# A fused two-layer image network on one core: the last phase's norm terms made in four rounds a unit

## The chip, the cores and the metric

The kernel runs on one core of a Trainium2 chip. The metric is the device time of one execution in microseconds (us), lower is better. TensorE (PE) does matrix products and transposes, VectorE (DVE) and ScalarE (ACT) work on tiles of 128 partitions, GpSimd (POOL) does small work beside them, and SyncE (SP) issues the DMAs. Each engine runs its own instructions in order; engines wait for each other by semaphores.

## The reference, cut to what matters

The input is an image batch of 8 x 96 channels x 128 x 128. The function has two layers, each of them a mixing part and a token-wise feed-forward part:

```
# layer 0
x = x + cluster_mixing(ln_c(x))                      # pooled centres, similarities
t = tokens(x);  t = t + ffn0(ln_t(t));  x = image(t)
# layer 1
n = ln_c(x) * gamma + beta                           # norm over the 96 channels
y = conv1x1(conv5x1(conv1x5(conv3x3(n))))            # depthwise, then 96x96
x = x + y * n
t = tokens(x)                                        # 131072 tokens of 96 channels
t = t + ffn1(ln_t(t))                                # output
# ln_t(v) = (v - mean) / sqrt(var + 1e-5), over the 96 channels of a token
# ffn(v): fp8 (5,2) rounded input and weights, 96 -> 384, + b1, relu,
#         rounded to fp8, 384 -> 96, + b2
```

The change touches only the norm `ln_t` ahead of the last feed-forward. For each token it needs a factor `rstd = (var + eps) ** -0.5` and an offset `shift = -mean * rstd`; the normalised token is `x * rstd + shift`.

## The kernel before, in words

The program has three phases, one after the other. Phase A does layer 0 and the norm of layer 1, phase B the depthwise convolutions, and phase C (function `phase_c`, names beginning `C_` in the profile) the rest: the 1x1 convolution, the product, the residual, and the second feed-forward. Only phase C is changed.

Phase C cuts the work into 32 units (`NQ`), each a quarter of one image, 4096 tokens. A unit is 32 tiles of 128 tokens (`NT`), in 8 groups k = 0 to 7 (`NK`) of 4 tiles each (`TPC`). The code of every engine walks over steps. In a step, unit i goes through the feed-forward, and unit q = i + 1 goes through the front part: convolution (`mix`, PE), product (`gate`, DVE), transpose to tokens (`turn`, PE), residual (`x4`, DVE, tile `C_xT`), statistics (`stats`, DVE, the BATCH_NORM_STATS2 of L178, tile `C_st`). A step has nine slots s = 0 to 8. The order on each engine is written out by hand in its `body`. With its names in the profile, what one slot s holds is:

- PE: `pe_q8(s+1)` (transpose of the normalised tokens, L1519), two thirds of `pe_hidden(s)` (L357), `mix(s)` (L1738), the last third of `pe_hidden(s)`, `pe_y(s-1)` (L1533), `turn(s-1)` (L1747), `c_turn(s-1)` (L1757).
- ACT: `act_q8(s+1)` (C_q8c, L305), three `act_hidden(s)` (C_h, L370), one group of the norm `act_norm` (C_q, L1504, four instructions, one for each tile), `act_y(s-1)` (C_y, L1546).
- DVE: `dve_hidden(s)` (C_hq, three of L378 and one of L382), `gate(s)` (L1822), `x4(s-1)` (L1832), `dve_y(s-1)` (C_y16b, L1552), `stats(s-1)` (L178, two), `out(s-1)` (C_outq, L1851).

Which group ACT normalises in which slot stands in a table. Groups 0, 1 and 2 of the next unit are normalised in slots 6, 7 and 8 of a step, groups 3 to 7 in slots 0 to 4 of the following one, and slot 5 has none:

```
LN_AT = {6: (1, 0), 7: (1, 1), 8: (1, 2), 0: (0, 3), 1: (0, 4), 2: (0, 5), 3: (0, 6), 4: (0, 7)}
```

POOL has one task in phase C, `norm_terms(q, half)`: from the statistics of half a unit (16 tiles, groups 0 to 3 or 4 to 7) it makes `rstd` and `shift`. It waits until DVE has finished the statistics of the half's last group (semaphore `bn2`), until ACT has used up the half's terms of the unit before (`norm2`), and for its own round before (`ln2`). Then it issues four instructions that depend on each other: var (L1891), less (L1892), pow (L1895, tile `C_rstd`), and shift (L1898). The last raises `ln2`. ACT waits for `ln2` ahead of groups 0 and 4, and DVE ahead of the statistics of groups 0 and 4 (they overwrite what the round of the unit before has read). The statistics of group 3 come in slot 4 of a step, those of group 7 in slot 8, the last one. So the terms of the second half can be started only as the step ends, and ACT reads them in slot 1 of the next step.

A counter `passed` is raised by POOL and ACT behind each such wait; nobody waits for it. SP loads the image rows (`C_x3q`, `C_y3q`) three steps ahead and the tokens (`C_xT`) two steps ahead.

Of the kernel before, what the change touches and what calls it, by code (L numbers as in the profile page):

```python
# [11 lines left out]
ALU = mybir.AluOpType  # L12
# [4 lines left out]
B, C, H, W = 8, 96, 128, 128  # L17
# [5 lines left out]
NT = TOK // P  # L23
NK = 8
TPC = NT // NK
# [7 lines left out]
EPS_T = 1e-5  # L33
# [71 lines left out]
def begun(unit):  # L105

    return unit.real
# [68 lines left out]
def pair_stats(dve, st, x, n):  # L176

    return dve.bn_stats(st[:, n:n + 2, :].rearrange("p t s -> p (t s)"),  # L178
                        x[:, n * C:(n + 2) * C].rearrange("p (t c) -> p c t", t=2))
# [1299 lines left out]
class RowFeedForward(SplitFeedForward):  # L1479
# [15 lines left out]

    def act_norm(self, act, i, k):
        ev = self.ev
        if k % 4 == 0:

            act.wait_ge(ev["ln2"], ev.at("ln2", i, k // 4))  # L1500
            act.sem_inc(ev.passed, 1)
        x = self.x_of(i)
        for t in range(k * TPC, (k + 1) * TPC):
            m = act.activation(self.q8[:, t, :], x[:, t * C:(t + 1) * C], ACT.Identity,  # L1504
                               scale=self.rstd[:, t:t + 1], bias=self.shift[:, t:t + 1], saturate=False)
        m.then_inc(ev["norm2"], 1)
# [108 lines left out]
def phase_c(nc, bufs, y3_dram, out_dram):  # L1615
# [3 lines left out]
    with ExitStack() as ctx:  # L1619
# [3 lines left out]
        for s in range(FFN_SLOTS):  # L1623
# [6 lines left out]
            if s >= 1:  # L1630
                front_uses.append(("turn", s - 1, 1, "x1", s - 1))
                back_uses += [("y", s - 1, 0, "y16", s - 1), ("c", s - 1, 0, "out", s - 1)]
        ev = Events(nc, ctx, "C_", dict(x1=NK, bn2=NK, ln2=2, ln2_s=6, norm2=NK, q8_full=NK, y_full=NK, c_full=NK, q8c=NK,
                                        hidden=NJ * NK, h16=NJ * NK, relu=NK, hq=NK, y16=NK, yb=NK, out=NK, pw_full=NK,
                                        turn_full=NK, gate=NK, out_st0=1, out_st1=1))
        NB, HR = LastBuffers.NB, RB // 2
# [3 lines left out]
        cst, idb, pw, expo, var, less = bufs.cst, bufs.idb, bufs.pw, bufs.expo, bufs.var, bufs.less  # L1640
# [4 lines left out]
        ff = RowFeedForward(nc, ctx, "C_", ev, back, xT_flat, wts, idb)  # L1645

        def group(plane, k):

            return plane[0:C, (k // 2) * 8:(k // 2) * 8 + 8, (k % 2) * QS:(k % 2) * QS + QS]
# [7 lines left out]
        def rows(flat):  # L1657

            return flat.rearrange("c (r w) -> c r w", w=QS)

        def steps(eng, body):
            for n in range(-1, NQ):
                body(Unit(0, n, 4, NQ - 1))
# [140 lines left out]
        @block.vector  # L1804
        def _(dve):
            dve.wait_ge(setup, 32)
            dve.tensor_copy(idb[:], cst[:]).then_inc(setup_dve, 1)
            dve.memset(expo[:], -0.5).then_inc(setup_dve, 1)
            ffn_dve(dve)

            def gate(q, k):

                dve.wait_ge(ev["pw_full"], ev.at("pw_full", q, k))
                if k == 0:

                    dve.wait_ge(ld_x[q.buf(2)], (q.round(2) + 1) * 16)

                if k >= 2:
                    dve.wait_ge(ev["turn_full"], ev.at("turn_full", q, k - 2))
                elif begun(q - 1):  # L1820
                    dve.wait_ge(ev["turn_full"], ev.at("turn_full", q - 1, NK - 2 + k))
                dve.tensor_tensor(rows(gated[:, k % 2, :]), rows(front.bank("pw", k)[0:C, 0:CH])[:, ::-1, :],  # L1822
                                  group(x3q[q.buf(2)], k), ALU.mult).then_inc(ev["gate"], 1)

            def x4(q, k):
                if k == 0:

                    dve.wait_ge(ld_t[q.buf(NB)], (q.round(NB) + 1) * 32)

                dve.wait_ge(ev["turn_full"], ev.at("turn_full", q, k))  # L1830
                v = xT[q.buf(NB)][:, k, :]
                dve.tensor_tensor(v, front.bank("turn", k)[:, 0:CW], v, ALU.add).then_inc(ev["x1"], 1)  # L1832

            def stats(q, k):
                if k % 4 == 0 and begun(q - 1):

                    dve.wait_ge(ev["ln2"], ev.at("ln2", q - 1, k // 4))
                dve.wait_ge(ev["x1"], ev.at("x1", q, k))
                for t in range(0, TPC, 2):
                    m = pair_stats(dve, ff.st, ff.x_of(q), k * TPC + t)  # L1840
                m.then_inc(ev["bn2"], 1)

            def out(i, k):
                if k % 4 == 0 and begun(i - 1):

                    n = f"out_st{k // 4}"
                    dve.wait_ge(ev[n], ev.at(n, i - 1, 0) * 16)

                dve.wait_ge(ev["c_full"], ev.at("c_full", i, k))
                dve.wait_ge(ev["yb"], ev.at("yb", i, k))  # L1850
                dve.tensor_tensor(group(outq, k), rows(back.bank("c", k)[0:C, 0:CH]), rows(ff.y16b[:, k % 2, :]),  # L1851
                                  ALU.add).then_inc(ev["out"], 1)

            def body(i):
                q = i + 1
                for s in range(FFN_SLOTS):
                    if i.real and s < NK:
                        ff.dve_hidden(dve, i, s)
                    if q.real and s < NK:
                        gate(q, s)  # L1860
                    if q.real and s >= 1:
                        x4(q, s - 1)
                    if i.real and s >= 1:
                        ff.dve_y(dve, i, s - 1)
                    if q.real and s >= 1:
                        stats(q, s - 1)
                    if i.real and s >= 1:
                        out(i, s - 1)

            steps(dve, body)  # L1870

        @block.gpsimd
        def _(pool):
            pool.wait_ge(setup_dve, 2)

            def norm_terms(q, half):

                n = NT // 2
                o = half * n
                pool.wait_ge(ev["bn2"], ev.at("bn2", q, 4 * half + 3))  # L1880
                pool.sem_inc(ev.passed, 1)
                if begun(q - 1):

                    pool.wait_ge(ev["norm2"], ev.at("norm2", q - 1, 4 * half + 3))
                    pool.sem_inc(ev.passed, 1)

                earlier = q if half else q - 1
                if begun(earlier):
                    pool.wait_ge(ev["ln2"], ev.at("ln2", earlier, 1 - half))
                    pool.sem_inc(ev.passed, 1)  # L1890
                pool.tensor_scalar(var[:], ff.st[:, o:o + n, 2], 1.0 / C, EPS_T, ALU.mult, ALU.add).then_inc(ev["ln2_s"], 1)  # L1891
                pool.tensor_scalar(less[:], ff.st[:, o:o + n, 1], -1.0, 0.0, ALU.mult, ALU.add).then_inc(ev["ln2_s"], 1)  # L1892
                pool.wait_ge(ev["ln2_s"], ev.at("ln2_s", q, 3 * half + 1))
                pool.sem_inc(ev.passed, 1)
                pool.tensor_tensor(ff.rstd[:, o:o + n], var[:], expo[:, 0:n], ALU.pow).then_inc(ev["ln2_s"], 1)  # L1895
                pool.wait_ge(ev["ln2_s"], ev.at("ln2_s", q, 3 * half + 2))
                pool.sem_inc(ev.passed, 1)
                pool.tensor_tensor(ff.shift[:, o:o + n], less[:], ff.rstd[:, o:o + n], ALU.mult).then_inc(ev["ln2"], 1)  # L1898

            def body(i):  # L1900
                q = i + 1
                for half in range(2):
                    if q.real:
                        norm_terms(q, half)

            steps(pool, body)


def metaformer_kernel(nc, x, consts, wf_t, wf, bf, wv_t, bv, wp_t, bp, alpha, beta, w1_0, b1_0, w2_0, b2_0,
                      gamma, beta_ln, dw13, valid, dwb, pw_t, w1_1, b1_1, w2_1, b2_1, out):  # L1910
    x2_dram = nc.dram_tensor("x2_scratch", [NQ, P, NK * CW], F32, kind="Internal").ap()
    x3_dram = nc.dram_tensor("x3_scratch", [C, B, H, W], F32, kind="Internal").ap()
    y3_dram = nc.dram_tensor("y3_scratch", [C, B, H, W], F32, kind="Internal").ap()
    strip_dram = nc.dram_tensor("strip_scratch", [C, 3, TAPW], F32, kind="Internal").ap()
    edge_dram = nc.dram_tensor("edge_scratch", [C, 2, 3, P], F32, kind="Internal").ap()
    phase_a(nc, consts, x, wf_t, wf, bf, wv_t, bv, wp_t, bp, alpha, beta, w1_0, b1_0, w2_0, b2_0,
            gamma, beta_ln, dw13, strip_dram, edge_dram, x2_dram, x3_dram)
    with ExitStack() as ctx:
        bufs = LastBuffers(nc, ctx, consts, pw_t, w1_1, b1_1, w2_1, b2_1, x2_dram, x3_dram)
        phase_b(nc, valid, dwb, strip_dram, edge_dram, x3_dram, y3_dram, bufs)  # L1920
        phase_c(nc, bufs, y3_dram, out)
# [54 lines left out]
```

## Time and profile before

| | us |
|---|---|
| median of 3 runs | 3664.3 (3664.11 to 3664.59) |
| the profiled execution, its own time | 3659.49 |
| its span in the trace | 3657.6 |
| busy: DVE, PE, ACT, POOL | 3218.4, 3017.4, 2781.3, 1728.9 |

The page also has the whole span in 40 slices. Phase C fills the last 12 of them: DVE and ACT are busy 90% or more in nearly all of those, PE 80%, POOL 20%. The chain that ended last, over the whole span, passes through ACT for 16%, through DVE for 4% and through POOL for 4%; the POOL part is the pow (C_rstd, L1895, 3%) with what stands around it. A busy share says how full an engine is on average; which wait ends last in a place has to be read from the timeline and the chain there.

### The profile page before, as it was taken

What the parts mean: (1) busy time and instruction counts of PE and PEld (TensorE: products, weight loads), DVE (VectorE), ACT (ScalarE), POOL (GpSimd) and SP (SyncE); (2) the same over time, 40 slices, a digit from 0 to 9 for tenths busy, and PEclk for the clock granted to TensorE, in tenths of its full rate; (3) what the DMA queues carried; (4) which work ended last, traced back from release to release, by engine and by line L of the source; (5) the groups of instructions that cost most, each with busy time, mean ns of one, the idle gap of its engine ahead of it and who ended that gap; (6) DMA issues with size and microseconds to landing.
All of it is one profiled execution on the core that took longest, in us unless ns stands there. A gap on an engine that the chain in (4) does not pass through costs nothing. (4 is left out here: it accounts for less than half of the span.)

```text
span 3657.6 us, 68122 instructions
## 1 busy us (share of the span) xinstructions
PE 3017.4 (82%) x21990; PEld 1910.0 (52%) x21990; DVE 3218.4 (88%) x8131; ACT 2781.3 (76%) x6274; POOL 1728.9 (47%) x2404
## 2 busy tenths in 40 slices
PE   6787888878787878887876799997888888888887
PEld 5565665656565656565654344443444444444444
DVE  4888889898989898989886699999899999999998
ACT  2577777777777877777778455554799999999998
POOL 3777777777787877787864000000222222222221
PEclk9999999899999999999987899999999999999999
DMA  3233323232323232323212888897676667666762
GB/s 68 53 89 74 91 71 88 71 88 70 88 71 88 71 88 71 88 71 88 71 56 69 212 238 234 236 280 212 172 199 188 181 185 200 184 184 193 199 177 83
DMA packets 696178, 478.92 MB, mean 131 GB/s; under 512 B 407217, under 2 KB 674422, under 8 KB 683830
## 3 DMA queue, kind: packets, MB, share of 16 engines
q1 hardware_dynamic: 695830, 474.58, 49.2%
q8 instruction: 182, 2.98, 0.3%
q14 instruction: 166, 1.36, 0.1%
HBM read 272.09 MB, written 201.92 MB: 130 GB/s over the span
## 5 line engine op out<-in xcount | busy, mean ns | idle before, releaser
L1891 POOL TENSOR_SCALAR C_var<-C_st 128x16 f32<-128x16 f32 x64 | 13.5, 211 | 1338.6 <-DVE C_st L178 1338.6
L1464 DVE SCALAR_TENSOR_TENSOR B_y<-B_mid,B_coefs,B_y 128x512 f32<-128x512 f32 x768 | 509.0, 750 | 3.2 <-ACT B_y L1429 3.2
L1395 PE MATMUL B_ps_row<-B_z,B_band 128*128 128x512 f32 x1152 | 499.1, 596 | 15.1 <-DMA B_band<-edge_scratch 15.1
L378 DVE TENSOR_SCALAR A_hq<-A_h,A_b 128x512 f16<-128x512 f16 x768 | 319.4, 456 | 176.5 <-ACT A_h L370 169.6
L370 ACT ACTIVATE A_h<-A_hid 128x512 f16<-128x512 f32 x768 | 428.3, 594 | 59.5 <-PE A_hid L357 57.1
L178 DVE BATCH_NORM_STATS2 A_st<-A_xT 128x6 f32<-128x192 f32 x1536 | 443.6, 349 | 29.3 <-ACT A_xT L861 16.0
L370 ACT ACTIVATE C_h<-C_hid 128x512 f16<-128x512 f32 x768 | 425.0, 589 | 22.9 <-PE C_hid L357 22.5
L1504 ACT ACTIVATE C_q<-C_xT,C_shift,C_rstd 128x96 fp8e5<-128x96 f32 x1024 | 392.6, 457 | 43.3 <-POOL C_shift L1898 43.2
L894 ACT ACTIVATE A_xc<-A_xT,A_shift,A_rstd 128x96 f32<-128x96 f32 x1024 | 379.3, 456 | 4.2 <-POOL A_shift L1207 4.0
L167 POOL TENSOR_TENSOR A_rstd<-A_var,A_expo 128x16 f32<-128x16 f32 x128 | 376.5, 2941 | 10.7
L1395 PEld LDWEIGHTS B_ps_row<-B_z,B_band 128*128 128x128 f32 x1152 | 218.8, 190 | 294.2 <-issue 287.8
L1738 PE MATMUL C_fbank<-C_y3q,C_pw 96*96 96x512 f32 x512 | 279.1, 627 | 77.7 <-DVE C_gated L1822 53.5
L357 PE MATMUL C_hid<-C_q8c,C_w 96*128 96x512 bf16 x768 | 259.3, 385 | 86.7 <-ACT C_h L370 83.4
L1420 ACT ACTIVATE B_mid<-B_ps_row,B_row_bias 128x512 f32<-128x512 f32 x192 | 130.4, 689 | 250.4 <-DVE B_y L1464 184.2
L297 PE MATMUL A_bbank<-A_w,A_hq 128*128 128x96 f16 x3072 | 192.6, 218 | 136.1 <-DVE A_hq L382 77.3
L357 PE MATMUL A_hid<-A_q8c,A_w 96*128 96x512 bf16 x768 | 267.3, 402 | 41.9 <-ACT A_h L370 39.5
L690 PEld LDWEIGHTS A_fbank<-A_big_w,A_xq 97*128 97x128 f32 x2048 | 275.9, 201 | 44.2 <-DVE A_pabd L1081 26.5
L690 PE MATMUL A_fbank<-A_big_w,A_xq 97*128 97x112 f32 x2048 | 282.2, 284 | 19.0 <-DVE A_pabd L1081 17.4
L378 DVE TENSOR_SCALAR C_hq<-C_h,C_b 128x512 f16<-128x512 f16 x768 | 243.7, 348 | 49.0 <-ACT C_h L370 38.9
L781 PE MATMUL A_fbank<-A_pabd,A_simT 128*128 128x384 f32 x512 | 244.0, 608 | 33.6 <-DVE A_xT L1088 33.6
L297 PEld LDWEIGHTS A_bbank<-A_w,A_hq 128*128 128x128 f16 x3072 | 165.5, 105 | 191.5 <-DVE A_hq L382 114.5
L305 ACT ACTIVATE A_q8c<-A_bbank 96x512 bf16<-96x512 f32 x256 | 149.3, 583 | 107.9 <-PE A_bbank L267 106.6
(167 smaller groups left out, 7248.7 us busy)
## 6 DMA issues: line engine op xcount, KB each, us to landing
A_xq<-in_x SPq DMA_DIRECT2D x32, 1536.0 KB, 8.9
x_scratch<-A_xT SPq DMA_DIRECT2D x64, 768.0 KB, 3.2
x_scratch<-A_x3h SPq DMA_DIRECT2D x64, 768.0 KB, 5.4
B_z<-x_scratch SPq DMA_DIRECT2D x96, 512.0 KB
y_scratch<-B_y SPq DMA_DIRECT2D x96, 512.0 KB, 3.6
C_x3q<-x_scratch SPq DMA_DIRECT2D x32, 1536.0 KB, 9.1
C_xT<-x_scratch SPq DMA_DIRECT2D x64, 768.0 KB, 16.6
C_y3q<-y_scratch SPq DMA_DIRECT2D x31, 1536.0 KB, 15.6
```

Of the source, the lines that this page charges most:

```text
L167: m = pool.tensor_tensor(rstd[:, o:o + n], var[:], expo[:, 0:n], ALU.pow)
L178: return dve.bn_stats(st[:, n:n + 2, :].rearrange("p t s -> p (t s)"), x[:, n * C:(n + 2) * C].rearrange("p (t c) -> p c t", t=2))
L297: m = pe.matmul(bank[:, t * C:(t + 1) * C], self.hq[:, b, s:s + P], self.w["w2"][:, j, :], start=(j == 0), stop=(j == NJ - 1))
L357: pe.matmul(self.hid2[n % 2][:], self.w["w1"][:, j * P:(j + 1) * P], self.q8c[:, k % 2, :], start=True, stop=True).then_inc(ev["hidden"], 1)
L370: act.activation(self.h16[:, k % 2, j * CH:(j + 1) * CH], self.hid2[n % 2][:], ACT.Copy).then_inc(ev["h16"], 1)
L378: r = dve.tensor_scalar(self.hq[:, b, s], self.h16[:, b, s], self.w["b1"][:, j:j + 1], 0.0, ALU.add, ALU.max)
L690: m = pe.matmul(bank[:, t * BIGN:(t + 1) * BIGN], xq[q.buf(NX)][:, n * P:(n + 1) * P], big_w[:, :], start=True, stop=True)
L894: m = act.activation(xc3[:, k // 4, t % (NT // 2), :], xT[u.buf(NB)][:, t * C:(t + 1) * C], ACT.Identity, scale=rstd3[:, t:t + 1], bias=sh ...
L1395: m = pe.matmul(bank(c, h), band[c.buf(NB)][:, d, :], z[c.buf(NB)][:, half(h), d:d + W], start=(d == 0), stop=(d == 2))
L1464: dve.scalar_tensor_tensor(y, mid[c.buf(2)][:, half(h), t:t + W], coefs[:, c.n, 3 + t:4 + t], y, ALU.mult, ALU.add).then_inc(ev["sums"], 1)
L1504: m = act.activation(self.q8[:, t, :], x[:, t * C:(t + 1) * C], ACT.Identity, scale=self.rstd[:, t:t + 1], bias=self.shift[:, t:t + 1], sa ...
L1738: pe.matmul(rows(front.bank("pw", k)[0:C, 0:CH]), pw[:], flipped(y3q[q.buf(2)], k), start=True, stop=True).then_inc(ev["pw_full"], 1)
```

## The change

A round of POOL makes the terms of two groups (8 tiles) in place of four (16 tiles), so there are four rounds a unit in place of two. Each round waits for the statistics of its own two groups only, and ACT and DVE wait for quarters: ahead of groups 0, 2, 4 and 6. The instructions of a round are the same four on half as many elements. The order of the work on ACT, DVE and PE stays as it was.

```diff
--- before.py
+++ after.py
@@ -1495,9 +1495,9 @@
 
     def act_norm(self, act, i, k):
         ev = self.ev
-        if k % 4 == 0:
-
-            act.wait_ge(ev["ln2"], ev.at("ln2", i, k // 4))
+        if k % 2 == 0:
+
+            act.wait_ge(ev["ln2"], ev.at("ln2", i, k // 2))
             act.sem_inc(ev.passed, 1)
         x = self.x_of(i)
         for t in range(k * TPC, (k + 1) * TPC):
@@ -1630,7 +1630,7 @@
             if s >= 1:
                 front_uses.append(("turn", s - 1, 1, "x1", s - 1))
                 back_uses += [("y", s - 1, 0, "y16", s - 1), ("c", s - 1, 0, "out", s - 1)]
-        ev = Events(nc, ctx, "C_", dict(x1=NK, bn2=NK, ln2=2, ln2_s=6, norm2=NK, q8_full=NK, y_full=NK, c_full=NK, q8c=NK,
+        ev = Events(nc, ctx, "C_", dict(x1=NK, bn2=NK, ln2=4, ln2_s=12, norm2=NK, q8_full=NK, y_full=NK, c_full=NK, q8c=NK,
                                         hidden=NJ * NK, h16=NJ * NK, relu=NK, hq=NK, y16=NK, yb=NK, out=NK, pw_full=NK,
                                         turn_full=NK, gate=NK, out_st0=1, out_st1=1))
         NB, HR = LastBuffers.NB, RB // 2
@@ -1832,9 +1832,9 @@
                 dve.tensor_tensor(v, front.bank("turn", k)[:, 0:CW], v, ALU.add).then_inc(ev["x1"], 1)
 
             def stats(q, k):
-                if k % 4 == 0 and begun(q - 1):
-
-                    dve.wait_ge(ev["ln2"], ev.at("ln2", q - 1, k // 4))
+                if k % 2 == 0 and begun(q - 1):
+
+                    dve.wait_ge(ev["ln2"], ev.at("ln2", q - 1, k // 2))
                 dve.wait_ge(ev["x1"], ev.at("x1", q, k))
                 for t in range(0, TPC, 2):
                     m = pair_stats(dve, ff.st, ff.x_of(q), k * TPC + t)
@@ -1873,35 +1873,37 @@
         def _(pool):
             pool.wait_ge(setup_dve, 2)
 
-            def norm_terms(q, half):
-
-                n = NT // 2
-                o = half * n
-                pool.wait_ge(ev["bn2"], ev.at("bn2", q, 4 * half + 3))
+            def norm_terms(q, part):
+
+
+                n = 2 * TPC
+                o = part * n
+                pool.wait_ge(ev["bn2"], ev.at("bn2", q, 2 * part + 1))
                 pool.sem_inc(ev.passed, 1)
                 if begun(q - 1):
 
-                    pool.wait_ge(ev["norm2"], ev.at("norm2", q - 1, 4 * half + 3))
+                    pool.wait_ge(ev["norm2"], ev.at("norm2", q - 1, 2 * part + 1))
                     pool.sem_inc(ev.passed, 1)
 
-                earlier = q if half else q - 1
+                earlier = q if part else q - 1
                 if begun(earlier):
-                    pool.wait_ge(ev["ln2"], ev.at("ln2", earlier, 1 - half))
+                    pool.wait_ge(ev["ln2"], ev.at("ln2", earlier, (part - 1) % 4))
                     pool.sem_inc(ev.passed, 1)
-                pool.tensor_scalar(var[:], ff.st[:, o:o + n, 2], 1.0 / C, EPS_T, ALU.mult, ALU.add).then_inc(ev["ln2_s"], 1)
-                pool.tensor_scalar(less[:], ff.st[:, o:o + n, 1], -1.0, 0.0, ALU.mult, ALU.add).then_inc(ev["ln2_s"], 1)
-                pool.wait_ge(ev["ln2_s"], ev.at("ln2_s", q, 3 * half + 1))
+                v, l = var[:, 0:n], less[:, 0:n]
+                pool.tensor_scalar(v, ff.st[:, o:o + n, 2], 1.0 / C, EPS_T, ALU.mult, ALU.add).then_inc(ev["ln2_s"], 1)
+                pool.tensor_scalar(l, ff.st[:, o:o + n, 1], -1.0, 0.0, ALU.mult, ALU.add).then_inc(ev["ln2_s"], 1)
+                pool.wait_ge(ev["ln2_s"], ev.at("ln2_s", q, 3 * part + 1))
                 pool.sem_inc(ev.passed, 1)
-                pool.tensor_tensor(ff.rstd[:, o:o + n], var[:], expo[:, 0:n], ALU.pow).then_inc(ev["ln2_s"], 1)
-                pool.wait_ge(ev["ln2_s"], ev.at("ln2_s", q, 3 * half + 2))
+                pool.tensor_tensor(ff.rstd[:, o:o + n], v, expo[:, 0:n], ALU.pow).then_inc(ev["ln2_s"], 1)
+                pool.wait_ge(ev["ln2_s"], ev.at("ln2_s", q, 3 * part + 2))
                 pool.sem_inc(ev.passed, 1)
-                pool.tensor_tensor(ff.shift[:, o:o + n], less[:], ff.rstd[:, o:o + n], ALU.mult).then_inc(ev["ln2"], 1)
+                pool.tensor_tensor(ff.shift[:, o:o + n], l, ff.rstd[:, o:o + n], ALU.mult).then_inc(ev["ln2"], 1)
 
             def body(i):
                 q = i + 1
-                for half in range(2):
+                for part in range(4):
                     if q.real:
-                        norm_terms(q, half)
+                        norm_terms(q, part)
 
             steps(pool, body)
```

## Rows read from the trace of the kernel before

**Rows 1.** Windows view, steady stretch of phase C: engines busy (instructions), clock, DMA.

```profile
2617.80:3623.30 1005.50, 847.26 (x4799) 463.79 (x4798) 937.45 (x2398) 958.89 (x2159) 232.09 (x240) 1.00 0.66 183
```

**Rows 2.** The same view, one step of the steady stretch.

```profile
3264.32:3297.82 33.50, 28.27 (x162) 15.46 (x161) 31.27 (x81) 31.98 (x73) 7.71 (x8) 1.00 0.69 191
```

**Rows 3.** Waits view: total us, times, longest; then line L1504: us, times.

```profile
ACT C_q L1504 <- POOL C_shift L1898: 43.2, 31, 31.7
...
  POOL C_shift L1898: 11.5, 30
```

**Rows 4.** Timeline, ACT, slots 1, 2: start, us, instruction [idle before <-releaser].

```profile
3291.85 1.66 ACT L370 ACTIVATE C_h<-C_hid 128x512 f16<-128x512 f32 x3
3293.87 1.54 ACT L1504 ACTIVATE C_q<-C_xT,C_shift,C_rstd 128x96 fp8e5<-128x96 f32 x4 [0.35 <-POOL C_shift L1898]
3295.31 0.57 ACT L1546 ACTIVATE C_y<-C_bbank 96x512 f16<-96x512 f32 x1
...
3296.27 1.66 ACT L370 ACTIVATE C_h<-C_hid 128x512 f16<-128x512 f32 x3
3297.82 1.53 ACT L1504 ACTIVATE C_q<-C_xT,C_shift,C_rstd 128x96 fp8e5<-128x96 f32 x4
```

**Rows 5.** The chain that ended last: start us, us, what, from slot 5 on.

```profile
3309.16 0.60 ACT C_h L370
...
3309.80 0.38 DVE C_hq L378
...
3315.24 1.10 PE C_fbank L1738 x2
...
3323.76 3.09 POOL C_rstd L1895
```

**Rows 6.** Timeline, DVE: slots 1, 6 and 7.

```profile
3295.01 0.54 DVE L1832 TENSOR_TENSOR C_xT<-C_fbank,C_xT 128x384 f32<-128x384 f32 x1
3295.92 0.35 DVE L1552 TENSOR_SCALAR C_y16b<-C_y,C_b 96x512 f16<-96x512 f16 x1 [0.37 <-ACT C_y L1546]
...
3313.12 0.87 DVE L378 TENSOR_SCALAR C_hq<-C_h,C_b 128x512 f16<-128x512 f16 x3
...
3316.95 0.87 DVE L378 TENSOR_SCALAR C_hq<-C_h,C_b 128x512 f16<-128x512 f16 x3
```

**Rows 7.** Timeline, POOL: two rounds and the start of a third.

```profile
3289.58 0.50 POOL L1892 TENSOR_SCALAR C_less<-C_st 128x16 f32<-128x16 f32 x1
...
3309.32 0.29 POOL L1892 TENSOR_SCALAR C_less<-C_st 128x16 f32<-128x16 f32 x1
...
3322.79 0.21 POOL L1891 TENSOR_SCALAR C_var<-C_st 128x16 f32<-128x16 f32 x1 [9.62 <-DVE C_st L178]
```

**Rows 8.** Instruction groups of POOL by shape: busy us, mean ns, idle before.

```profile
L1895 POOL TENSOR_TENSOR C_rstd<-C_var,C_expo 128x16 f32<-128x16 f32 x64 | 191.9, 2998 | 11.7 <-POOL C_less L1892 11.7
...
L1231 POOL TENSOR_TENSOR A_cpow<-A_cn,A_expo 96x4 f32<-96x4 f32 x32 | 41.9, 1308 | 73.4 <-DVE A_cn L1164 73.4
```

**Rows 9.** Timeline, ACT, slot 6.

```profile
3312.76 0.60 ACT L370 ACTIVATE C_h<-C_hid 128x512 f16<-128x512 f32 x1 [0.39 <-PE C_hid L357]
3313.30 1.54 ACT L1504 ACTIVATE C_q<-C_xT,C_shift,C_rstd 128x96 fp8e5<-128x96 f32 x4
```

**Rows 10.** Timeline of the phase's first step; two stretches of the windows view.

```profile
2578.43 2.98 ACT L1504 ACTIVATE C_q<-C_xT,C_shift,C_rstd 128x96 fp8e5<-128x96 f32 x8 [31.69 <-POOL C_shift L1898]
...
2580.12 0.63 PE L1519 MATMUL C_bbank<-C_idb,C_q 128*96 128x128 bf16 x4 [1.78 <-ACT C_q L1504]
...
2581.42 0.56 DVE L1832 TENSOR_TENSOR C_xT<-C_fbank,C_xT 128x384 f32<-128x384 f32 x1 [1.56 <-PE C_fbank L1747]
...
2575.00:2579.00 4.00, 2.83 (x12) 1.38 (x12) 3.73 (x9) 0.56 (x2) 3.12 (x2) 1.00 0.02 4
...
2581.00:2583.00 2.00, 1.83 (x10) 1.15 (x9) 1.18 (x3) 2.00 (x7) 0.07 (x1) 0.50 0.97 229
```

**Rows 11.** One line's instructions in the steady stretch: duration in ns, min/median/max.

```profile
L382 DVE TENSOR_SCALAR C_hq<-C_hq x240: 559/560/561, 2619.3 to 3619.4; 128x1536 uint16<-128x1536 uint16 x120
```

## The prediction

> **What bounds the kernel now.** I read the windows view first. A row gives, behind the length of the stretch, the busy time of PE, PE's weight load, DVE, ACT and POOL. In the steady part of phase C, 1005.5 us and 30 of the 32 steps, ACT is busy 958.89 us (95%) and DVE 937.45 us (93%), PE 84%, POOL 23%, the clock is full and the DMA queues 66% used [rows 1]. The reader should see two engines near their limit and no third. One step takes 33.50 us, of which ACT works 31.98 and DVE 31.27 [rows 2]. So 1.52 us of a step are ACT's idle time, and the question is how much of it is POOL's doing.
>
> The waits view names it: ACT waited for the shift of POOL 31 times, 43.2 us. One of them is the wait at the phase's start, 31.7 us, most of which is loading. The other 30, one a step, are 11.5 us or 0.38 us each [rows 3].
>
> An idle number is not yet a loss. The timeline shows what the wait costs ACT: in slot 1 the three C_h start at 3291.85 and the four C_q behind them at 3293.87, 2.02 us later. In slot 2 the same two groups stand 1.55 us apart (3296.27, 3297.82) [rows 4]. The difference is 0.47 us: 0.35 idle, and 0.12 because consecutive ACT instructions overlap and after a wait they can't.
>
> Last the chain of waits, to see whether that 0.47 lies on the path. Each step repeats one pattern. ACT runs without a gap from slot 1 to the last C_h of slot 5 (3309.16); DVE takes over at 3309.80 for two slots; PE's mix at 3315.24 hands back to ACT; slot 8 passes over DVE's statistics to POOL's pow (3323.76) and then to ACT's slot 1 [rows 5]. So every step passes once through POOL's round, and the round starts only when the statistics of group 7 end.
>
> **The change, part by part.**
>
> The second half's wait goes. Groups 4 and 5 will need the statistics of group 5, not of group 7. POOL's two rounds begin at about 3309.0 (group 3 done, its second instruction at 3309.32) and 3322.79 (group 7 done) [rows 7]. DVE's slots are 3.83 us apart (3313.12, 3316.95) [rows 6]. Group 5 therefore ends two slots ahead of group 7 less the shorter slot 8, at about 3316.5. ACT reads the terms of group 4 in slot 1, at 3293.87 + 33.50 = 3327.37 now, or 3326.90 without the wait. That leaves 10.4 us for a round which now takes 4.5 (3322.79 to 3327.27). The wait is gone, whatever the shorter pow costs.
>
> The price of a shorter round is not in this trace for 8 elements. Pow takes 3.00 us on 128x16 and 1.31 us on 96x4 [rows 8]. These two are the ends; a straight line between them gives 1.31 + 4 x 1.69/12 = 1.87 us, which I take, as 8 lies nearer to 4. With the three small instructions a round is then some 3.3 us, four of them 13 us of POOL's 33. Even at 4.5 us a round they fit: rounds are triggered at the ends of slots 2, 4, 6 and 8, 7.7 us or more apart save the last pair, which is about 6.
>
> The other new waits. Groups 0 and 1 (slots 6 and 7) now wait for the statistics of slot 2, group 2 (slot 8) for slot 4, group 6 (slot 3 of the next step) for slot 8. The shortest distance is from slot 4 to slot 8 and from slot 8 to slot 3, about 10 us each less one round. Behind ACT's wait stands everything ACT does, so a late round would cost its lateness in full; none is late. POOL's first wait for ACT (terms of the unit before used up) asks for reads that lie 5 or more slots back. DVE's new waits ahead of groups 2 and 6 ask for a round of the unit before, a step old: nothing.
>
> Two more wait-and-count pairs a step on ACT. In slot 6 the pair stands ahead of C_q today: the last C_h starts at 3312.76 and is 0.60 long, C_q starts at 3313.30, 0.54 behind and before that C_h has ended [rows 9]. Without a pair the step from an instruction to the next is 0.49 to 0.53 (three C_h and the following C_q in 1.55 us, [rows 4], is 0.52 each). So a pair costs between nothing and 0.05; below nothing is excluded, as nothing is removed. At worst a drained hand-over, 0.12 each, 0.24 a step. I take nothing.
>
> The gain of 0.47 has to survive what follows. With C_q at 3293.40, C_y of slot 1 comes at 3294.84 in place of 3295.31 and ends at 3295.41. DVE waits there now, 0.37 us, and starts at 3295.92; its work before (C_xT at 3295.01) lets the next begin some 0.46 later, at 3295.47 [rows 4, 6]. So DVE moves 0.45 earlier, and this is all the slack it had: from here on a DVE slot of 3.83 us stands against 3.95 for ACT (3293.87 to 3297.82), which ACT sets, as before, and slots 5 to 7 are DVE's, shifted with the rest. I take 0.47; the next limit would be DVE's own 31.27 us, 1.8 us below the new step of 33.03 us.
>
> 30 steps x 0.47 = 14.1 us. The last unit, where PE is late too, counts nothing.
>
> The first step. ACT's first C_q comes at 2578.43, when the round of groups 0 to 3 has ended; PE waits 1.78 us for it, until 2580.12, and since its transposes for group 7 stand behind, DVE waits 1.56 us, until 2581.42 [rows 10]. After the change the round of groups 0 and 1 starts two of these short slots (1.9 us each) sooner and is shorter. Both waits go, and PE does its eight transposes one group behind the other: I take 2.0 us, between 1.56 (DVE's wait) and 3.4. The upper end is this: PE's granted clock is 1.00 (2.4 GHz) in 2575 to 2579 and 0.50 (1.2 GHz) in 2581 to 2583 [rows 10]. It fell while PE waited; if it stays up, up to another 1.4 us goes.
>
> Sum: 14.1 + 2.0 = 16.1 us. On the profiled execution, 3659.49 becomes 3643.4. That execution lies 4.8 us below the median of the runs, 3664.3; for the median, 3664.3 - 16.1 = 3648.2.
>
> A rule that speaks against the change: the Trainium skill, "GPSIMD Engine Reference", section "Key points", says that GpSimd shares its SBUF interfaces with VectorE and contends with DVE instructions in a two-port mode or with two SBUF inputs. In the trace the contention shows on POOL's side: the same C_less takes 0.50 us beside DVE's C_hq and 0.29 without [rows 7]. By the rule the other way round, DVE would lose some tenths for each of POOL's now 16 small works a step; it is a rival below.
>
> **The rivals.**
>
> A. The ACT pairs cost a drained hand-over each, 0.24 a step. Then 30 x 0.23 + 2.0 = 8.9 us, 3655.4. Against it: the 0.54 of [rows 9].
>
> B. The step stays at 33.5 us because another chain is as long: DVE has next to no slack after slot 1, as computed above. PE's mix, which waits for DVE, could hold the last third of C_h in slot 2. Then only the first step gains, 3662.3. For it: the match within 0.02 us. Against it: the numbers still come out on the good side.
>
> C. Slower: POOL's new round beside slots 3 and 4 delays DVE where it has only 0.12 us a slot to spare. If each of the four instructions of that round costs DVE 0.3 us (what C_less loses to DVE is 0.21), DVE is 1.2 late less 0.24 slack, 0.96 against a gain of 0.47: +0.49 x 30 - 2.0 = 12.7 us, 3677. It decides from a delay of 0.7 us a step. Against it: the rounding instruction of DVE, which works in SBUF alone, lasts 559 to 561 ns in all 240 cases of the steady stretch [rows 11], though today's rounds (9 us of 33.5) lie beside some of them.
>
> D. More than forecast: the clock stays up in the first step and the pipeline gives back up to 0.50 a step: 15.0 + 3.4 = 18.4 us, 3645.9. It is the upper part of the forecast's own range.
>
> That the change does nothing (rounds as long as before, so POOL falls behind) has no room: four rounds of 4.5 us are 18 of 33 us.
>
> **How the numbers follow.** Forecast with D 0.80, A 0.09, B 0.07, C 0.04. The time is the forecast's, 3648.2. The forecast's own range is 3645 to 3651; to A it reaches 3655.5, and with a spread between executions of a few us I give 3644.5 to 3656. Faster by over 0.2% (7.3 us, about what a measurement of this kernel can tell from no change) is forecast, D, and most of A: 0.87. Within 0.2% is B and the rest of A: 0.10. Slower: 0.03.
>
> **What would show it.** In the profile after: pow 128 times at 1.3 to 3.0 us (1.9 expected); no row of ACT C_q waiting for POOL save the first; C_h to C_q in slot 1 at 1.55; DVE's wait in slot 1 near nothing; a step of 33.0 us; POOL gone from the chain; the first C_q some 4 to 5 us sooner. Wrong would be: a step of 33.5 with the POOL wait gone (B), ACT gaps ahead of the C_q of groups 2 and 6 (A), or longer DVE instructions beside POOL's (C).

## The result, and the profile after

| | before | after |
|---|---|---|
| runs of the first comparison, us | 3664.07, 3664.11, 3664.3, 3664.59 | 3638.38, 3639.03, 3645.08, 3645.69 |
| median | 3664.2 | 3642.06 |
| the profiled execution | 3659.49 | 3645.08 |

The change makes the kernel faster: the ratio after / before is 0.9942, 95% interval 0.993 to 0.9954. In a second comparison the same two kernels gave 3639.77 (5 runs) against 3659.91 us (21 runs, 3653.96 to 3663.06), a ratio of 0.9951, 0.9938 to 0.9963. The predicted time, 3648.2 with a range of 3644.5 to 3656, was too high: the measured 3642.06 lies below the range.

The two profiled executions lie 14.4 us apart (3659.49 - 3645.08), the two medians 22.1. So there are two questions: whether the mechanism was the one forecast, and where the rest comes from.

The waits view of the changed kernel's last phase (us in total, times, longest) answers to [rows 3]:

```profile
ACT C_q L1504 <- POOL C_shift L1900: 27.7, 1, 27.7
...
ACT C_h L370 <- PE C_hid L357: 23.4, 64, 0.4
...
ACT C_q8c L305 <- PE C_bbank L1519: 19.8, 32, 7.4
...
DVE C_y16b L1552 <- ACT C_y L1546: 10.3, 36, 1.0
```

POOL is waited for once, at the start, where ACT now waits 27.7 us in place of 31.7. The 30 waits of the steady part are gone. What ACT still waits for is PE: 23.4 us over 64 times in front of C_h, about 0.37 each.

One step of the windows view (PE, weight load, DVE, ACT, POOL busy; clock; DMA share; GB/s), against [rows 2]:

```profile
3238.88:3271.91 33.03, 28.27 (x161) 15.47 (x161) 31.20 (x81) 31.83 (x74) 9.76 (x16) 1.00 0.69 191
```

The step is 33.03 us, forecast 33.03. ACT's and DVE's work is the same as before within 0.2 us. POOL is busy 9.8 us in place of 7.7.

ACT's timeline in slots 1 and 2 of one step, against [rows 4] (start, us, instruction, idle before):

```profile
3217.51 1.53 ACT L1504 ACTIVATE C_q<-C_xT,C_shift,C_rstd 128x96 fp8e5<-128x96 f32 x4
3218.94 0.58 ACT L1546 ACTIVATE C_y<-C_bbank 96x512 f16<-96x512 f32 x1
...
3219.90 1.67 ACT L370 ACTIVATE C_h<-C_hid 128x512 f16<-128x512 f32 x3
3221.46 1.53 ACT L1504 ACTIVATE C_q<-C_xT,C_shift,C_rstd 128x96 fp8e5<-128x96 f32 x4
```

No idle time stands ahead of the C_q of slot 1 (3217.51). From it to that of slot 2 (3221.46) it is 3.95 us, as before from slot to slot.

DVE's timeline of slot 1 in the same step, against [rows 6]:

```profile
3216.57 0.84 DVE L378 TENSOR_SCALAR C_hq<-C_h,C_b 128x512 f16<-128x512 f16 x2 [0.84 <-ACT C_h L370]
...
3219.11 0.54 DVE L1832 TENSOR_TENSOR C_xT<-C_fbank,C_xT 128x384 f32<-128x384 f32 x1
3219.58 0.34 DVE L1552 TENSOR_SCALAR C_y16b<-C_y,C_b 96x512 f16<-96x512 f16 x1
```

C_y16b follows C_xT 0.47 later with no wait, where it waited 0.37 us. The forecast said 0.46.

POOL's timeline of a whole round, and the start of the one before and behind it:

```profile
3213.37 0.20 POOL L1893 TENSOR_SCALAR C_var<-C_st 128x8 f32<-128x8 f32 x1 [2.96 <-DVE C_st L178]
...
3224.79 0.20 POOL L1893 TENSOR_SCALAR C_var<-C_st 128x8 f32<-128x8 f32 x1 [8.38 <-DVE C_st L178]
3225.07 0.29 POOL L1894 TENSOR_SCALAR C_less<-C_st 128x8 f32<-128x8 f32 x1
3225.54 1.64 POOL L1897 TENSOR_TENSOR C_rstd<-C_var,C_expo 128x8 f32<-128x8 f32 x1 [0.18 <-POOL C_less L1894]
3227.36 0.20 POOL L1900 TENSOR_TENSOR C_shift<-C_less,C_rstd 128x8 f32<-128x8 f32 x1 [0.18 <-POOL C_rstd L1897]
3232.69 0.20 POOL L1893 TENSOR_SCALAR C_var<-C_st 128x8 f32<-128x8 f32 x1 [5.13 <-DVE C_st L178]
```

A round takes 2.77 us (3224.79 to 3227.56; some 3.3 were forecast), and the pow on 128x8 is 1.64 us (forecast 1.87, between 1.31 and 3.00). The chain of the changed kernel from slot 5 to slot 1 of the next step, against [rows 5]:

```profile
3232.81 0.61 ACT C_h L370
...
3233.44 0.37 DVE C_hq L378
...
3238.88 1.10 PE C_fbank L1738 x2
...
3243.22 1.43 ACT C_q L1504 x4
...
3245.53 1.31 ACT C_h L370 x3
...
3247.09 1.53 ACT C_q L1504 x4
3248.62 0.48 ACT C_q8c L305
```

It goes from DVE through PE's mix to ACT and stays on ACT. POOL has left it.

### The profile page after: what moved, and what is told of

It reads as the page before. It is cut to its first block and busy times, and to the rows that moved or that the text cites. A ratio compares the mean times of both kernels' runs of the same rounds, so it can differ in the third digit from the quotient of the medians.

```text
span 3643.0 us, 68822 instructions
## 1 busy us (share of the span) xinstructions
PE 3024.2 (83%) x21990; PEld 1917.1 (53%) x21990; DVE 3214.9 (88%) x8131; ACT 2778.0 (76%) x6274; POOL 1795.7 (49%) x2660
## 5 line engine op out<-in xcount | busy, mean ns | idle before, releaser
L1893 POOL TENSOR_SCALAR C_var<-C_st 128x8 f32<-128x8 f32 x128 | 26.3, 205 | 1231.1 <-DVE C_st L178 1231.1
L178 DVE BATCH_NORM_STATS2 A_st<-A_xT 128x6 f32<-128x192 f32 x1536 | 443.8, 350 | 27.6 <-ACT A_xT L861 14.4
L370 ACT ACTIVATE C_h<-C_hid 128x512 f16<-128x512 f32 x768 | 425.5, 590 | 23.6 <-PE C_hid L357 23.4
L1504 ACT ACTIVATE C_q<-C_xT,C_shift,C_rstd 128x96 fp8e5<-128x96 f32 x1024 | 391.8, 457 | 27.7 <-POOL C_shift L1900 27.7
## 6 DMA issues: line engine op xcount, KB each, us to landing
C_xT<-x_scratch SPq DMA_DIRECT2D x64, 768.0 KB, 16.5
```

Source lines behind the costliest of these rows:

```text
L370: act.activation(self.h16[:, k % 2, j * CH:(j + 1) * CH], self.hid2[n % 2][:], ACT.Copy).then_inc(ev["h16"], 1)
```

## The experiments

T is the theory of the prediction, with what the result adds: the steady gain is the round taken off the path, and the rest lies in the phase's first step, where PE's clock matters. Its rivals are named in each expectation. To set all traces side by side I use two measures taken from ACT's and PE's timelines: the step (from one C_q of slot 1 to the next), and the first stretch (from PE's first mix of phase C to the first C_q of slot 1).

| kernel | median, us (runs) | ratio to before, 95% | step | first mix at | first stretch | clock in it |
|---|---|---|---|---|---|---|
| before | 3664.2 (4) | | 33.50 | 2562.85 | 26.32 | 1.00, then 0.50 |
| after | 3642.06 (4) | 0.993 to 0.9954 | 33.04 | 2560.49 | 29.22 | 0.50 |
| e1 after again | 3639.77 (5) | 0.9938 to 0.9963 | 33.03 | 2567.09 | 23.17 | 1.00 |
| e4 before again | 3659.36 (11) | 0.999 to 1.0008 | 33.50 | 2563.40 | 29.22 | 0.50 |
| e2 second half split | 3646.6 (5) | 0.9945 to 0.9973 | 33.04 | 2562.33 | 29.22 | 0.50 |
| e3 first half split | 3657.63 (11) | 0.9987 to 1.0005 | 33.48 | 2561.77 | 23.18 | 1.00 |
| e5 after, warmed | 3639.53 (5) | 0.9932 to 0.9957 | 33.04 | 2561.60 | 21.35 | 1.00 |
| e6 before, warmed | 3658.01 (11) | 0.9985 to 1.0003 | 33.50 | 2558.40 | 24.50 | 1.00, then 0.50 |
| e7 long rounds | 3642.8 (4) | 0.9938 to 0.9967 | 33.04 | 2557.64 | 29.23 | 0.50 |
| e8 more waits | 3643.14 (4) | 0.9935 to 0.9965 | 33.03 | 2560.46 | 29.22 | 0.50 |
| e9 other table | 3607.87 (4) | 0.9844 to 0.9871 | 31.83 | 2563.10 | 27.91 | 0.50 |
| e10 table, warmed | 3601.83 (4) | 0.9828 to 0.9855 | 31.83 | 2562.53 | 20.17 | 1.00 |
| e11 table, halves | 3821.52 (4) | 1.0424 to 1.0459 | 38.6 | 2566.03 | 30.02 | 0.50 |

The last columns are of the profiled execution alone. The clock column leaves out the first 4 us, whose mean is 0.50 to 0.55 in all but the warmed ones. The first stretches of e9, e10 and e11 belong to another table of slots and compare only among themselves. The step of e11 is a mean: its 31 steps are 37.8 to 39.8 us long and take 1195.7 us in all.

**e1: the changed kernel once more.** No edit.

> The changed kernel once more, for a second trace and more times. Theory T (extra 6 us are a matter of PE's clock in the first step of phase C and of where phases A and B ended, not of the change): the times again fall into two groups, near 3638.5 and 3645.3, and the profiled execution, if it is of the lower group, has PE's granted clock at 1.00 from about 4 us after the first mix on, and a distance from the first mix to the first C_q of slot 1 of 24 to 25 us (29.2 in the first trace). Rival R (the steady step is shorter in the faster executions): the step is below 33.0 us. Ratio to before 0.993 to 0.995.

Measured: the five times are 3638.93, 3639.14, 3639.77 and 3645.24, 3645.72, two groups again. The profiled execution had the high clock and a first stretch of 23.17 (24 to 25 expected), 6.05 us shorter than in the first trace. But at 3645.24 it is one of the slower ones, against T, since its phase C began 6.6 us later. So the clock of the first step is confirmed as a cost of 6 us, R falls (step 33.03), and the two groups of times aren't explained by that clock alone: phase A varies too. Phase B and the gap behind it take 525.9 us in both traces (phase B's first product at 2034.58 and 2041.18). The times of e7 and e8, whose steps are those of the changed kernel, fall between the two groups as well.

The windows view of four traces in this stretch, first the changed kernel's two (3 to 7 us behind the first mix, then 16 to 20), low and high:

```profile
2565.00:2569.00 4.00, 3.80 (x8) 1.77 (x9) 2.95 (x7) 0.00 (x0) 0.00 (x0) 0.50 1.14 258
2577.00:2581.00 4.00, 3.86 (x9) 1.43 (x8) 2.24 (x6) 0.00 (x0) 0.76 (x4) 0.50 0.02 4
```

```profile
2571.00:2575.00 4.00, 3.04 (x15) 1.41 (x13) 3.73 (x9) 0.00 (x0) 0.21 (x1) 1.00 0.98 226
2583.00:2587.00 4.00, 3.03 (x19) 1.61 (x20) 2.92 (x9) 4.00 (x10) 3.07 (x5) 1.00 0.86 213
```

The granted clock is 0.50 (1.2 GHz) throughout in the one and 1.00 (2.4 GHz) in the other. At the low level PE is busy 3.80 and 3.86 of 4 us, so PE sets the pace of the first stretch and everything behind it is waiting; at the high level it is busy 3.04.

**e4: the kernel before once more.** No edit.

> The kernel before under a name of its own, for a second trace. T: its executions too fall into two groups, one near 3659.5 (clock at 1.00 in the first step soon after the first mix) and one near 3664.3 (clock late); a trace of the slower group has 4 to 5 us more between the first mix and the first C_q of slot 1 (26.3 in the first trace). Rival R2: the 4.8 us between its profiled execution and its timed runs lie in phases A or B: the first mix comes that much later.

Measured: 3653.49 to 3663.38 in 11 runs, spread evenly and not in two groups. Its trace has the low clock and a first stretch of 29.22, 2.9 more than the first trace of before (4 to 5 expected). Its first mix comes 0.55 us later (R2), so neither T's size nor R2 alone accounts for the 3.9 us between the two executions:

```profile
2565.00:2569.00 4.00, 3.77 (x9) 1.50 (x8) 2.49 (x5) 0.00 (x0) 0.00 (x0) 0.50 1.15 269
2577.00:2581.00 4.00, 3.77 (x8) 1.40 (x7) 2.35 (x6) 0.00 (x0) 3.02 (x3) 0.50 0.00 0
```

At the low clock the kernel before and the changed one need the same 29.22 us. The change gains nothing there, since PE, busy 3.77 of 4 us, is the bound and neither POOL's round nor ACT's first C_q is.

**e5 and e6: PE kept busy ahead of the first mix.** The same edit in the changed kernel and in the one before:

```diff
             pe.wait_ge(setup, 32)
+            for _ in range(14):
+                pe.matmul(back.banks[0][:, 0:P], cst[:], cst[:], start=True, stop=True)
             pe.wait_ge(setup_dve, 2)
```

> The changed kernel, and PE does 14 products that nobody reads (identity by identity, into a bank not yet in use) between the start of phase C and its first mix. T: PE's granted clock is then 1.00 from the first mix on in every execution; first mix to first C_q of slot 1 in 22 to 23.2 us (29.2 with the low clock, 23.2 in the trace with the high one); the times lose the slower 6 us of the first step; step 33.04. Rival: the clock stays low all the same, the distance stays 29.2 or varies.

> The same 14 products in the kernel before. T: the clock is up at the first mix, falls where PE waits for ACT's first C_q as in the first trace; first mix to first C_q of slot 1 in 25 to 26.3 us. The difference to e5 in this distance, 3 us, is the change's gain in the first step at the high clock (forecast 2.0); in low-clock executions it is 0 (both 29.2). Step 33.50. Rival: with the clock up to stay, PE's wait costs only 1.6 to 2.0 us as forecast, and the distance is 25.2.

Measured: with the products the clock is at 1.00 from the first mix on in both traces. In e5 it stays there; in e6 it falls to 0.50 behind PE's wait for ACT's first C_q (1.78 us, until 2573.86; the clock is down from 2574.2 on):

```profile
2563.00:2567.00 4.00, 3.20 (x14) 1.44 (x13) 3.75 (x9) 0.00 (x0) 0.00 (x0) 1.00 1.11 258
2575.00:2579.00 4.00, 2.96 (x25) 1.78 (x22) 3.19 (x8) 3.48 (x9) 2.78 (x7) 1.00 0.68 168
```

```profile
2568.00:2572.00 4.00, 3.01 (x16) 1.44 (x13) 3.74 (x9) 0.00 (x0) 3.48 (x4) 1.00 0.00 0
2576.00:2580.00 4.00, 4.00 (x12) 1.61 (x11) 1.19 (x5) 3.56 (x9) 3.33 (x3) 0.50 1.00 225
```

The first stretches are 21.35 (22 to 23.2 expected) and 24.50 (25 to 26.3), so both were a little shorter than expected, and the change gains 3.15 us there when the clock is up, the same as e1 against the first trace of before (26.32 - 23.17). The forecast of this term was 2.0, and the rival of e6 falls. Between the medians, 3639.53 and 3658.01, lie 18.5 us. The sum from the traces is 15.2 + 3.15 = 18.4. The five times of the warmed kernel lie within 2.5 us (3637.97 to 3640.45), none near 3645. Its median is only 0.2 us below that of e1, so the medians don't show what the warm-up is worth in the changed kernel. The first stretch is 1.8 us shorter than with the high clock of e1 and 7.9 shorter than with the low one. The products themselves delay the first mix: it comes 527.4 (e5), 526.6 (e6) and 527.9 us (e10) after phase B's first product, against 525.5 to 526.7 in the ten other traces. e6 against before is not told apart from no change.

**e2 and e3: one half of the change at a time.** Rounds on groups 0-3, 4-5, 6-7 (e2) and on 0-1, 2-3, 4-7 (e3). The edit, cut to its core:

```diff
+PARTS = [(0, 4), (4, 6), (6, 8)]      # e3: [(0, 2), (2, 4), (4, 8)]
-                n = 2 * TPC
-                o = part * n
+                g0, g1 = PARTS[part]
+                n = (g1 - g0) * TPC
+                o = g0 * TPC
```

The waits of ACT, DVE and POOL follow the parts.

> Three rounds: groups 0 to 3 as before (16 tiles), groups 4-5 and 6-7 as quarters. T: the whole steady gain is here, the step is 33.03 us; the first step keeps DVE's and PE's waits for the round of groups 0 to 3 (1.6 and 1.8 us at full clock), so 2 us slower than the changed kernel at the same clock. 3640 to 3649. Rival: the round of groups 0 to 3, which ends 0.1 us before ACT's C_q in slot 6, becomes the path in the shorter step, and the step is 33.1 or more.

> Three rounds: groups 0-1 and 2-3 as quarters, groups 4 to 7 as before (16 tiles). T: the step stays at 33.50 with ACT's 0.35 us wait for POOL in slot 1; only the first step gains, 2 us: 3657 to 3664. Rival: a part of the steady gain comes from the first half's quarters, and the step is clearly below 33.5.

Measured: e2 has the step of 33.04, e3 that of 33.48 and the whole gain of the first stretch (23.18). In e3 the waits view of the steady part shows POOL's round back on the path:

```profile
ACT C_q L1508 <- POOL C_shift L1905: 11.7, 30, 1.2
```

In e2 nothing of it is left but one wait of 0.3 us. So the steady gain is the second half's, the first step's gain the first half's, as T has it. The 2 us that e2 was to lose in the first step can't be seen, as its trace has the low clock; its median, 3646.6, lies 6.8 above that of e1, with a spread of 5.6 us within its own five runs. The times of e3 alone don't show its gain (0.9987 to 1.0005). The rival of e2 (the first half's round comes onto the path in the shorter step) falls.

**e7: rounds of twice the length.** Each round makes a second pow on a scratch tile. The edit, cut to its core:

```diff
+                pool.tensor_tensor(scratch[:], expo2[:], expo[:, 0:NT // 2], ALU.pow).then_inc(ev["ln2_s"], 1)
+                pool.wait_ge(ev["ln2_s"], ev.at("ln2_s", q, 4 * part + 3))
```

> The changed kernel, and each of POOL's four rounds has a second pow, on 16 elements of a scratch tile that nobody reads, ahead of its last instruction: a round lasts 6 us in place of 2.7, POOL is busy some 23 of 33 us. T: the distance to ACT's reading is about 10 us, so nothing is late: step 33.04 to 33.06, 3638 to 3646. Rival C (POOL's work beside DVE slows it): DVE's instructions get longer and the step rises by some tenths.

Measured: the step is 33.04, with POOL busy 22.1 of 33 us. The windows view, one step:

```profile
3200.00:3233.04 33.04, 28.24 (x161) 15.51 (x160) 31.15 (x81) 31.83 (x73) 22.12 (x21) 1.00 0.70 190
```

and one line of DVE, duration in ns (min/median/max), against [rows 11]:

```profile
L382 DVE TENSOR_SCALAR C_hq<-C_hq x238: 559/560/587, 2620.5 to 3598.3; 128x1536 uint16<-128x1536 uint16 x119
```

DVE is busy 31.15 us a step, as in the changed kernel (31.20). The length of a round doesn't matter, and rival C falls: the median is the 560 ns of before, the longest of 238 is 587 against 561, and with more than twice the POOL time the step hasn't moved.

**e8: sixteen wait-and-count pairs a step on ACT, in place of four.**

```diff
-        if k % 2 == 0:
+        for _ in range(1 if k % 2 == 0 else 3):
             act.wait_ge(ev["ln2"], ev.at("ln2", i, k // 2))
             act.sem_inc(ev.passed, 1)
```

> The changed kernel, and ACT passes more wait-and-count pairs on the same, long fulfilled, values: three ahead of each odd group, so 16 pairs a step in place of 4. T: the pairs are passed while the instruction before still runs: step 33.04. Rival A: each costs a drained hand-over, 0.05 to 0.12 us, and the step rises by 0.6 to 1.4 us, 3658 to 3685.

Measured: step 33.03. Rival A falls: twelve more pairs cost nothing that the trace shows.

**e9 and e10: what the quarters allow.** After the change ACT's norm has 10 us to spare, and the chain alternates between ACT in slots 8 to 5 and DVE in slots 5 to 7. In slots 0 and 8 DVE has little to do, and ACT's free slot was 5:

```diff
-LN_AT = {6: (1, 0), 7: (1, 1), 8: (1, 2), 0: (0, 3), 1: (0, 4), 2: (0, 5), 3: (0, 6), 4: (0, 7)}
+LN_AT = {5: (1, 0), 6: (1, 1), 7: (1, 2), 8: (1, 3), 1: (0, 4), 2: (0, 5), 3: (0, 6), 4: (0, 7)}
```

> The changed kernel with another table of slots for ACT's norm: groups 0 to 3 of the next unit in slots 5 to 8, none in slot 0, groups 4 to 7 in slots 1 to 4. T: what sets the step after the change is that ACT is over-full in slots 8 and 0 (where DVE has little) and DVE in slots 5 to 7 (where ACT waits); with the free slot at 0 both engines fill alike, and the step falls to 31.7 to 32.3 us, 22 to 41 us in all: 3600 to 3620. Rival: DVE's and PE's order of work sets the step whatever ACT does, and it stays at 33.0.

> The table of e9 and the warm-up of e5 together. T: both gains add: the step as in e9, first mix to first C_q of slot 1 as in e5 or a little less; up to 6 us below e9's slower executions. Rival: none of its own.

Measured: the step falls to 31.83, and the gain in the first stretch comes on top of it (27.91 at the low clock, 20.17 warmed): 3607.87, and with the warm-up 3601.83 us, 1.6% below the kernel before (ratio 0.9842) and the best version here. The windows view of one step of e9, and its waits of ACT from 2600 us to the end of the phase:

```profile
3197.31:3229.14 31.83, 28.27 (x161) 15.47 (x160) 31.08 (x81) 31.60 (x74) 9.76 (x16) 1.00 0.70 197
```

```profile
ACT C_q8c L305 <- PE C_bbank L1519: 0.7, 1, 0.7
ACT C_y L1546 <- PE C_bbank L1533: 0.7, 1, 0.7
ACT C_h L370 <- PE C_hid L357: 0.4, 2, 0.2
```

ACT works 31.60 of 31.83 us. These three waits are 1.8 us in all; in the changed kernel those ahead of C_h alone were 23.4 over the whole phase. Now ACT is the bound in the plain sense.

**e11: the same table with the old halves.** The edit of e9 in the kernel before.

> The kernel before with its two rounds a unit, and the table of e9 (groups 0 to 3 of the next unit in slots 5 to 8, none in slot 0). T: the table needs the quarters: the terms of group 0 are ready only 3.5 us after ACT wants them in slot 5, so ACT waits there, and the step is 33.8 to 35.3 us, slower than before, 3670 to 3715. Rival: the table alone is what helps, and the step falls below 33.0 without the quarters.

Measured: 3821.52 us, 4.4% slower. The table needs the quarters. ACT's timeline:

```profile
3211.52 1.54 ACT L1504 ACTIVATE C_q<-C_xT,C_shift,C_rstd 128x96 fp8e5<-128x96 f32 x4 [1.55 <-POOL C_shift L1898]
...
3230.86 1.54 ACT L1504 ACTIVATE C_q<-C_xT,C_shift,C_rstd 128x96 fp8e5<-128x96 f32 x4 [3.45 <-POOL C_shift L1898]
```

It waits 1.55 us ahead of group 4 and 3.45 ahead of group 0, 5.0 a step where I had expected 3.5 in one place. The step is 38.6 in the mean, beyond the 33.8 to 35.3 expected. The direction is T's, the size was not. Set on e9's step of 31.83, the two waits would give 36.8 us, by estimate; some 1.7 us are left. PE's clock has a part in them: while ACT waits, PE waits for ACT, and its clock falls to 0.50 once or twice a step. Behind the wait at 3230.86 PE stands idle for 3.74 us, until 3233.89, and the clock is down from 3233.2 to 3240.1. The windows view of the steady part and of that stretch:

```profile
2620.00:3780.00 1160.00, 916.92 (x4811) 509.60 (x4810) 945.67 (x2405) 959.94 (x2165) 224.36 (x240) 0.93 0.57 160
3234.00:3240.00 6.00, 6.00 (x17) 3.22 (x17) 4.88 (x13) 3.91 (x9) 0.00 (x0) 0.50 0.01 3
```

The granted clock is 0.93 in the mean of 1160 us, where the kernel before has 1.00 [rows 1]. So the waits for POOL cost more than their own length here. How the 1.7 us divide between the slower PE and statistics that come late for the next round stays open.

## Why the prediction was wrong, point by point

Right, by its own steps:

- The 0.47 us a step. Step 33.03 forecast, 33.03 to 33.04 in every trace of the changed kernel. The mechanism, the place and the absorbed slack of DVE (0.46 forecast, 0.47 read) were as told.
- The costs put at nothing: ACT's pairs (e8), POOL's longer total (e7), DVE's new waits, the late rounds. Rivals A, B and C did not happen.
- The pow on 8 elements lay between its bounds, and its value made no difference.

Wrong, in three terms:

- "30 steps x 0.47 = 14.1 us". From the first C_q of slot 1 to the last, the kernel before takes 1039.76 us and the changed one 1024.54: 15.2 us, over 31 steps, the last of which gains only 0.25. Most of the missing 1.1 us are two steps of the kernel before that are longer than 33.50, the third by 0.83 and the sixteenth by 0.29. In the third, POOL's round itself was late. Its timeline:

```profile
2685.39 0.49 POOL L1891 TENSOR_SCALAR C_var<-C_st 128x16 f32<-128x16 f32 x1 [9.92 <-DVE C_st L178]
2685.96 0.34 POOL L1892 TENSOR_SCALAR C_less<-C_st 128x16 f32<-128x16 f32 x1
2686.49 3.27 POOL L1895 TENSOR_TENSOR C_rstd<-C_var,C_expo 128x16 f32<-128x16 f32 x1 [0.18 <-POOL C_less L1892]
2689.93 0.45 POOL L1898 TENSOR_TENSOR C_shift<-C_less,C_rstd 128x16 f32<-128x16 f32 x1 [0.18 <-POOL C_rstd L1895]
```

  The round takes 4.99 us in place of 4.5, and starts late as well; ACT waits 1.18 us for it. As these steps are the same in e4 and e6 (34.33 to 34.35 and 33.78 to 33.81), they are no accident of one execution. The third goes with the wait. In the sixteenth ACT's wait for POOL is the usual 0.36; it loses its time earlier, in slot 5, where DVE starts its statistics 0.28 us late (3110.97). Why it does, and why the changed kernel has no such step, stays open. I had read one step and multiplied it, and not looked at the longest.
- "I take 2.0 us, between 1.56 and 3.4", the first step. It is 3.15 us with the clock at its upper level and 0 with the lower one (29.22 before and after). I had treated the clock as an extra on top of the gain, when it decides whether there is a gain, because at 1.2 GHz PE is the bound of this stretch. The kernel before loses its high clock itself, by the wait that the change removes: it falls in the two traces that have the wait and the high clock (before, e6), and stays up in the four that have the high clock without the wait (e1, e3, e5, e10).
- "That execution lies 4.8 us below the median of the runs": I carried this difference over to the changed kernel as if it were a constant. It is a difference between executions. In the traces it lies wholly ahead of the first C_q of slot 1: from there to the end of the span the kernel before takes 1068.4 us in all three of its traces (before, e4, e6), and the changed one 1053.2 to 1053.3 in its own (after, e1, e5, e7, e8). What varies is the clock in the first step (up to 6.05 us for the changed kernel, 2.9 for the one before) and phase A, with whose end the first mix moves between 2557.64 and 2567.09 us over the 13 traces. This is the largest of the three: of the 6.1 us by which the forecast was too high, the two terms above give at most 2.3, and at least 3.8 lie in which executions the two medians were taken from. The changed kernel's profiled execution was near the top of its runs, that of the kernel before 4.8 below its own.

A reading that no term of the sum rests on, but rival C's price does, was wrong too: that C_less takes 0.50 us beside DVE's C_hq and 0.29 without [rows 7]. DVE's C_hq run beside both, each time from 0.16 to 0.17 us ahead of it on:

```profile
3289.41 1.02 DVE L378 TENSOR_SCALAR C_hq<-C_h,C_b 128x512 f16<-128x512 f16 x3
...
3309.16 1.00 DVE L378 TENSOR_SCALAR C_hq<-C_h,C_b 128x512 f16<-128x512 f16 x3
```

What sets the two apart is the round: in the steady part of the kernel before C_less of groups 4 to 7 takes 0.50 us in all but one of 30 cases, that of groups 0 to 3 0.28 to 0.29. Why stays open, and with it the 0.21 us that the forecast called the loss to DVE.

The account: 15.2 for the steady part, and between 0 and 3.15 for the first step at the same clock, makes 15.2 to 18.4 us; 16.1 was forecast, and that it lies in this range is in part luck, as one term was too low and the other is too high or too low with the clock. With unlike clocks the same terms give, by estimate, 12.3 us (26.32 against 29.22) to 21.3 (29.22 against 23.17). The medians of the kernels with these steps came out 22.1 (after), 20.1 (e1), 16.9 (e7) and 16.5 us (e8) below the kernel before. What the first comparison shows above 18.4 is in the size of the spread between executions: its four runs of before lie at 3664.1 to 3664.6, and only 2 of the 43 runs of that kernel in the later comparisons were as slow. How much of the remaining 4 us is phase A and how much the clock stays open, since only profiled executions show either. The range was too narrow at its lower end: it held the unknown costs, not the spread between executions, of which the 4.8 us were a warning.

## What to carry to other kernels

When one wait is on the path once per step, the gain is the step's difference times the number of steps, and here one step could be forecast to 0.01 us; look at the longest steps as well as at the usual one. A profiled execution and the timed runs can differ by more than the change's first-order uncertainty, so a range has to hold that spread. And a wait that is taken off the path can be worth more as room than as time: here it gave 0.46 us a step by itself, and 1.2 us more once ACT's work was moved into the slots where DVE is light, which without it would have cost 4.4%.

## What the runs showed of the hardware

- The clock at the start of phase C takes either course in the same kernel: 0.50 in the changed kernel's first trace from the first mix to 20 us behind it, though PE is busy 95% of the time (3.80 of 4 us), or 1.00 from about 4 us after the first mix (e1). What decides between them stays open. Fourteen idle products ahead of it gave 1.00 from the first mix in all three traces that had them.
- POOL's pow mostly takes 1.64 us on 128x8 (up to 2.05 in the changed kernel), 2.90 to 3.27 on 128x16 and 1.31 on 96x4. From 8 to 16 elements (1.64 to 2.90) each one adds 0.16 us; the 96x4 row doesn't lie on that line, which would give 1.01, so the straight line of the forecast gave 1.87.
- POOL's second small instruction (C_less) mostly takes 0.50 us in the round behind slot 8 and 0.20 to 0.29 in the others, in the kernel before (16 elements) as in the changed one (8), though DVE's C_hq lie beside it alike. DVE's rounding instruction keeps its 560 ns with POOL busy 7.7 or 22.1 us of a step.
- Where PE waits, its granted clock can fall: to 0.50 behind one wait of 1.78 us in the phase's first step (before, e6), and once or twice in every step of e11, where PE's waits last up to 3.74 us (mean 0.93).
